# The next tile's second gate/up pair at the end of a round, the decay masks later, and other filler products in the first round

## The chip, the cores and the metric

One NeuronCore of a Trainium2 chip runs one program. The metric is the device time of one execution in microseconds, median of several runs. TensorE is called PE in the views, VectorE DVE, ScalarE ACT, GpSimd POOL and SyncE SP.

## The reference

Two layers over 2 x 1024 tokens of 256 channels, all in float32. Cut to what matters:

```python
xn = layernorm(x)
s = rwkv_attention(xn)          # mixes w,k,v,r,g; decays exp(-exp(w)); recurrence over time per head; W_o
g = silu(down(sparsify_2to4(silu(xn @ w_gate) * (xn @ w_up))))     # of 4 neighbours the 2 largest |h| stay
x = x + s * g
xn = layernorm(x)
s = ssd(xn)                     # B, C, X and a residual gate; chunked scan with decays; w_out
g = silu(down(silu(xn @ w_gate1.T) * (xn @ w_up1.T)))
x = x + s * g
```

## The kernel before

The 2048 tokens are eight tiles of 256. The program runs nine **rounds**. In a round the first layer works on tile `a` and the second layer on the tile before it, `b`. The first round has only `a`, the last only `b`. Rounds two to seven are one hardware loop (`Fori`, line 359), round eight is the same code written out once more with the next tile left out, and `rounds` (line 356) calls `one(a, b)` of each engine. The order of the work on each engine is written by hand in that function, and the engines meet at semaphores.

**The hidden layer of tile `a`** has 1024 units in four pairs of blocks, p0 to p3. `project_p(a, n, "g")` and `"u"` are the gate and up products of pair n: four 128x256 products each, which the records show as eight, because a float32 product leaves two records. ACT makes silu of the gate (`ffn_tanh`, line 574) and DVE multiplies with the up product (`hidden`, line 889). For a pair that `whole` (line 303) doesn't name, ACT makes only a tanh, and DVE needs two instructions (lines 900 and 904) in place of one (896). Then ACT takes the absolute value (`ffn_abs`), DVE compares neighbours (`sparse_compare`, line 1085) and selects, and PE multiplies with the down weights (`down_0`, in the first round `down_part`, line 1540). In the loop, pair 0 of the next tile is made at the end of a round (`next_gate_0`, `next_up_0`), and pair 1 in the middle of the tile's own round, behind `carries`.

**The decays within a tile** are seven levels: `level_next` (line 972) on DVE scales keys and queries, PE multiplies them (`low_levels`, `high_levels`, line 1595), and DVE takes the products under a mask (`own_taken`, `low_taken`, `high_taken`: lines 992 to 1068). In the first round `level` and `level_step` do it step by step in place, and PE has so little to do between them that `kept_at_work` (line 1898) puts products there that nobody reads: one of 256 columns ahead of `level(a, 1)`, one ahead of `out_turned` and six ahead of `turned_1`.

**The second layer's decay rows** `cs_row` come back from DRAM by a DMA, and POOL masks them with an `affine_select` (line 553) that waits for that DMA alone. `end_args` on DVE and `L_exps` on ACT wait for the mask (`cs_masked`). ACT copies B and C into `BC` with sixteen instructions (`bc`, line 602).

**PSUM** has eight banks. `FILLS` (line 54) says which product comes into which bank in what order, `LAST_FILLS` and `FIRST_FILLS` for the last and first round. A product waits until the one ahead of it in its bank is freed. So the tables set which engine a product can wait for.

```python
def kept_at_work(name, count):
    open_bank(a, name)
    for _ in range(count):
        t_.matmul(ps(a, name)[:, 0:C], ident[:, :], W["f_gate"][:, 0:C], start=True, stop=True)
```

## Time and profile before

| what | value |
|---|---|
| runs | 735.85 us median of 3, 734.74 to 736.4 |
| profiled execution | 735.66 us, its span 733.9 us |
| PE | 711.3 us busy (97%), 6896 records |
| PE weight loads | 590.1 us (80%) |
| DVE, ACT, POOL | 497.5 (68%), 342.0 (47%), 77.2 us (11%) |
| mean granted PE clock | 0.995 of full speed |

The span runs from the first to the last instruction. The 1.8 us around it belong to the start and end of an execution. All times below are microseconds from the start of the span. PE's records overlap, so the start of one group to the start of the next is the better measure of its cost.

### The profile page before, as it was taken

Reading aid. Unit: us, or ns where it says so; the run is one execution under the profiler, and the core shown is the slowest. Engines: PE = TensorE matmul, PEld = TensorE weight load, DVE = VectorE, ACT = ScalarE, POOL = GpSimd, SP = SyncE. Lnnn points to the kernel's source line nnn. Section 1 sums busy time; section 2 is a strip of 40 time slices with the busy share of each in tenths; the row PEclk is TensorE's granted clock in tenths of the full one; section 3 lists DMA queues with packets and bytes.
Section 4 is the critical chain, followed back from the end, with each engine's and each line's share of the span. In section 5 each row is a group of like instructions: output and inputs, shape, how many; then the busy total and the mean of one; then the engine's idle time right before and its main releaser. Section 6 shows DMA issues by size and latency. Waiting matters only on the chain.

```text
span 733.9 us, 17949 instructions
## 1 busy us (share of the span) xinstructions
PE 711.3 (97%) x6896; PEld 590.1 (80%) x6896; DVE 497.5 (68%) x1207; ACT 342.0 (47%) x678; POOL 77.2 (11%) x85
## 2 busy tenths in 40 slices
PE   5998999999999999999999999999999999999998
PEld 3777688877888688886888868888788878888686
DVE  4976599547895478955787558855689547895133
ACT  1411685226832468215762168522584236821690
POOL 6301011101011010100111001110101101011020
PEclk9989999999999999999999999999999999999999
DMA  7900351125400353013531145102540136301360
GB/s 238 404 23 29 102 88 32 15 73 144 75 2 15 88 146 59 2 28 104 117 59 16 30 138 95 32 15 69 142 80 3 15 87 145 59 2 26 119 116 16
DMA packets 122444, 55.93 MB, mean 76 GB/s; under 512 B 104384, under 2 KB 114176, under 8 KB 120832
## 3 DMA queue, kind: packets, MB, share of 16 engines
q1 hardware_dynamic: 122368, 54.76, 30.3%
q8 instruction: 66, 1.08, 0.6%
q14 instruction: 10, 0.08, 0.0%
HBM read 42.35 MB, written 12.40 MB: 75 GB/s over the span
## 4 chain that ended last, share of the span: by engine, by line
PE 76%; DVE 12%; issue 5%; DMA 2%; SPq 2%; ACT 2%; POOL 1%; DVEq 0%; ACTq 0%; POOLq 0%
PE psum L1486 58%; PE psum L1707 2%; PE psum L1722 2%; PE psum L1514 2%; PE psum L1565 1%; PE psum L1760 1%; PE psum L1931 1%; PE psum L1595 1%; PE psum L1733 1%; DVE beats L1085 1%; PE psum L1577 1%; DVE own L992 1%; PE psum L1554 1%; PE psum L1873 1%; SPq L453 1%
## 5 line engine op out<-in xcount | busy, mean ns | idle before, releaser
L602 ACT ACTIVATE BC<-psum 64x256 f32<-64x256 f32 x128 | 81.4, 636 | 3.0 <-PE psum L1486 1.3
L1486 PE MATMUL psum<-xn1T,sb_n_gate 128*128 128x256 f32 x256 | 61.3, 382 | 0.0
L1486 PE MATMUL psum<-xn1T,sb_n_up 128*128 128x256 f32 x256 | 60.6, 380 | 0.4 <-DVE cs_row L1294 0.4
L1486 PE MATMUL psum<-xnT,sb_f_gate 128*128 128x256 f32 x240 | 58.5, 386 | 0.0
L1486 PE MATMUL psum<-xnT,sb_f_up 128*128 128x256 f32 x240 | 57.6, 382 | 0.0
L733 ACT ACTIVATE thFB<-psum 128x512 f32<-128x512 f32 x8 | 4.8, 597 | 104.9 <-PE psum L1486 104.9
L1486 PEld LDWEIGHTS psum<-xn1T,sb_n_up 128*128 128x128 f32 x256 | 48.0, 190 | 6.9 <-DVE cs_row L1294 0.8
L1486 PEld LDWEIGHTS psum<-xn1T,sb_n_gate 128*128 128x128 f32 x256 | 48.0, 190 | 6.8
L1486 PEld LDWEIGHTS psum<-xnT,sb_f_up 128*128 128x128 f32 x240 | 44.8, 190 | 6.4 <-issue 0.3
L1486 PEld LDWEIGHTS psum<-xnT,sb_f_gate 128*128 128x128 f32 x240 | 44.2, 189 | 6.8 <-issue 0.2
L1486 PE MATMUL psum<-sb_f_down,hid 128*128 128x256 f32 x224 | 49.5, 379 | 0.0
L1486 PE MATMUL psum<-sb_n_down,hidB 128*128 128x256 f32 x224 | 49.5, 379 | 0.0
L1486 PEld LDWEIGHTS psum<-sb_f_down,hid 128*128 128x128 f32 x224 | 42.6, 190 | 5.8
L1486 PEld LDWEIGHTS psum<-sb_n_down,hidB 128*128 128x128 f32 x224 | 42.6, 190 | 5.8
L553 POOL TENSOR_SCALAR_AFFINE_SELECT cs_row<-cs_row 128x2048 f32<-128x2048 f32 x8 | 16.5, 2062 | 225.7 <-DMA cs_row<-cs_dram 225.7
L628 ACT ACTIVATE cs_row<-cs_row,cs_col 128x128 f32<-128x128 f32 x128 | 38.9, 392 | 0.0
L559 POOL TENSOR_TENSOR cs_half<-cs_half,BC 128x1024 f32<-128x1024 f32 x8 | 18.9, 2363 | 169.5 <-ACT cs_half L697 169.5
L1085 DVE TENSOR_TENSOR beats<-habs 128x768 bf16<-128x768 f32 (+2 forms) x48 | 32.6, 719 | 0.4 <-ACT habs L589 0.4
L1486 PE MATMUL psum<-sb_w_X,xn1T 128*128 128x512 f32 x64 | 31.7, 618 | 0.0
L1486 PE MATMUL psum<-xn1T,sb_w_B 128*128 128x256 f32 x128 | 30.9, 385 | 0.2
L580 ACT ACTIVATE thB<-psum 128x512 f32<-128x512 f32 x32 | 18.8, 594 | 21.8 <-PE psum L1486 21.7
L1486 PE MATMUL psum<-xn1T,sb_w_C 128*128 128x256 f32 x128 | 28.9, 379 | 0.0
(257 smaller groups left out, 1459.0 us busy)
## 6 DMA issues: line engine op xcount, KB each, us to landing
cs_row<-cs_dram SPq DMA_DIRECT2D x8, 1024.0 KB, 4.9
x_dram<-gate SPq DMA_DIRECT2D x8, 512.0 KB, 2.8
cs_half<-cs_dram SPq DMA_DIRECT2D x16, 256.0 KB, 5.9
hidB<-x_dram SPq DMA_DIRECT2D x8, 512.0 KB, 5.9
b_dram<-B_turned SPq DMA_DIRECT2D x32, 128.0 KB, 3.3
hidB<-b_dram SPq DMA_DIRECT2D x8, 512.0 KB, 4.2
X<-in_x SPq DMA_DIRECT2D x9, 256.0 KB, 3.5
XT<-in_x_turned SPq DMA_DIRECT2D x8, 256.0 KB, 3.6
```

What stands on the lines that cost most here:

```text
L453: sp_.dma_start(to[s, e], B_turned[r:r + 32, :].rearrange("p (n d) -> p n d", d=32)).then_inc(B_stored, 16)
L553: g.affine_select(out=cs_row[:, :, :], in_=cs_row[:, :, :], compare_op=ALU.is_ge, fill=NEG, base=0, pattern=[[0, NQ * SCH], [1, P]], chann ...
L559: g.tensor_tensor(cs_half[:, :], cs_half[:, :], BC[:, 1, :, :].rearrange("p t h -> p (t h)"), ALU.mult).then_inc(Cdec_ready, 1)
L580: free(a_.activation(buf[:, :], ps(t, name + "g")[:, :], ACT.Silu), t, name + "g")
L602: ins = a_.activation(cols[:, par, 2 * pair:2 * pair + 2, :], src[64 * par:64 * par + 64, :, s, :], ACT.Identity)
L628: ins = a_.activation(cs_row[:, n, :], cs_row[:, n, :], ACT.Exp, bias=cs_col[:, n:n + 1])
L992: return d.copy_predicated(odd, masks[:, 0, :].rearrange("p (e g b) -> p e g b", e=2, b=32), data)
L1085: did(d.tensor_tensor(beats[:, first:first + count, :], habs[:, i:i + 1, :].to_broadcast([P, count, T]), habs[:, i + 1:4, :], ALU.is_ge))
L1486: ins = t_.matmul(ps(t, name)[first_row:first_row + rows, col:col + n], w, x, start=(k == 0), stop=(k == len(ws) - 1))
L1514: ins = t_.matmul(ps(t, name)[:, i * T:(i + 1) * T], W[w][:, c:c + P], xnT[:, h, 1:T + 1], start=(h == 0), stop=(h == CH - 1))
L1707: ins[s] = t_.matmul(ps(t, names[s])[:, i * P:(i + 1) * P], Bf[r, c * P:(c + 1) * P], Cf[r, c * P:(c + 1) * P], start=True, stop=True)
L1722: t_.matmul(y_out(t, s, c, par), Xrow[:, s, c, :], m[:, par, :], start=(c == 0), stop=(c == 0), skip_group_check=True)
```

## The change

It makes both products of pair 1 of the next tile at the end of a round, behind those of pair 0, also in the first round, where they stand in the place of six filler products. ACT makes silu of both pairs there (`next_gates`) and loads the table for exp, so DVE needs one instruction for pair 1. The bank tables give `p1g` and `p1u` the ends of banks 7 and 4, and `k` moves to bank 2. POOL's mask waits for `level_next(a, 3)` as well, `end_args` moves behind `B_by_block`, and ACT's `gate_tanh` behind the first half of `L_exps`. All three compares of the first half come early on DVE. On PE `res0` stands ahead of `gate_in`. In the first round the down products are cut in pairs of blocks and spread, and the fillers are 128 columns wide, four and nine of them. The differences and `xxxT` (`rank_inputs`) are two functions now, with `normed_1` between them in the first round. In the last round `B0` stands ahead of `carries`.

```diff
-         ["p0g", "mix_k", "w1", "p1g", "mix_g1", "L1", "M1", "kv", "p3u", "yT"],
+         ["p0g", "mix_k", "w1", "mix_g1", "L1", "M1", "kv", "p3u", "yT"],
...
-            return name not in ("p0", "p1", "p2") or (name == "p2" and t.first) or (name == "p0" and not t.first)
+            return name not in ("p0", "p1", "p2") or t.first == (name == "p2")
...
                     pool.wait_ge(cs_rows_loaded, b.count(16, 32))
                     pool.sem_inc(passed, 1)
+                    if a:
+                        pool.wait_ge(lev_ready, a.count(6, 4))
+                        pool.sem_inc(passed, 1)
...
+                def next_gates():
+                    for n in range(2):
+                        ffn_tanh(a.next(), f"p{n}", th[n], None)
+                    exp_tables()
...
                 if a and b:
-                    ffn_tanh(a, "p0", th[0], th_ready)
-                    exp_tables()
                     rank_tanh()
...
-                    gate_tanh()
                     end_exp()
                     L_exps(0)
+                    gate_tanh()
...
+                    if a.reg is not None:
+                        next_gates()
...
                     ffn_tanh_0()
+                    next_gates()
                     copy(a, xn1T[:, :, :], "xT1", CH)
...
                     hidden_p(a, 0)
+                    hidden_p(a, 1)
                     mix_scaled(a, "w")
...
-                    hidden_p(a, 1)
+                    compare(0)
                     mix_g_scaled(a)
                     mix_add(a, "g")
-                    sparse_compare(a, 0, 0)
...
-                    end_args()
                     B_by_block(0)
                     B_by_block(1)
+                    end_args()
...
                     res_gate(1)
-                    sparse_compare(a, 0, 1)
-                    sparse_compare(a, 0, 2)
                     B_decayed()
...
-                        t_.matmul(ps(a, name)[:, 0:C], ident[:, :], W["f_gate"][:, 0:C], start=True, stop=True)
+                        t_.matmul(ps(a, name)[:, 0:P], ident[:, :], W["f_gate"][:, 0:P], start=True, stop=True)
...
                     carries()
-                    project_p(a, 1, "u")
-                    project_p(a, 1, "g")
                     keys()
...
                     low_levels(a)
+                    ssd_proj(b, "res0", "w_res", 0)
                     gate_in()
-                    ssd_proj(b, "res0", "w_res", 0)
...
                         next_up_0()
+                        ffn_p(a.next(), 1)
...
-                    kept_at_work("p2u", 1)
+                    kept_at_work("p2u", 4)
...
-                    kept_at_work("yT", 1)
+                    kept_at_work("yT", 9)
...
                     next_up_0()
-                    kept_at_work("xT1", 6)
+                    ffn_p(a.next(), 1)
                     turned_1()
```

TensorE at the end of the first round, before and then of the change. `sb_f_gate` and `sb_f_up` with `xnT` are a pair's products, `ident` with `sb_f_gate` is the filler, `habs` the transposes of `turned_1`:

```order
L1486 MATMUL psum<-xnT,sb_f_up 128x256 x4
L1903 MATMUL psum<-sb_f_gate,ident 128x256 x6
L1554 MATMUL psum<-ident,habs 128x128 x4
L359 UNCONDITIONAL_BRANCH
L359 ISA
```

```order
L1500 MATMUL psum<-xnT,sb_f_up 128x256 x4
L1500 MATMUL psum<-xnT,sb_f_gate 128x256 x4
L1500 MATMUL psum<-xnT,sb_f_up 128x256 x4
L1568 MATMUL psum<-ident,habs 128x128 x4
L362 UNCONDITIONAL_BRANCH
```

The two groups of pair 1 stand where the six fillers stood.

TensorE in the loop round behind the decay product of the first layer (`decT`), before and then of the change. `prefix,before` is `carries`, `mixed_k` the keys, `mixed_v` the values:

```order
L1807 MATMUL psum<-decT,sb_dec 128x128 x4
L1486 MATMUL psum<-prefix,before 128x2
L1475 REGISTER_ALU
L1486 MATMUL psum<-xnT,sb_f_up 128x256 x4
L1486 MATMUL psum<-xnT,sb_f_gate 128x256 x4
L1813 REGISTER_ALU
L1486 MATMUL psum<-mixed_k,sb_w_rkvgo 128x256 x4
```

```order
L1821 MATMUL psum<-decT,sb_dec 128x128 x4
L1489 ISA
L1500 MATMUL psum<-prefix,before 128x2
L1827 REGISTER_ALU
L1500 MATMUL psum<-mixed_k,sb_w_rkvgo 128x256 x4
```

The pair's eight products have gone from between `carries` and the keys.

VectorE in the loop round from the end of `own_taken` (`same`) to `level_next(a, 4)`, before and then of the change. `B_turned` is `B_by_block`, and `cs_col` and `to_end` are `end_args`, which waits for the mask:

```order
L1068 COPY_PREDICATED own<-same,psum 128x256
L334 REGISTER_ALU
L334 REGISTER_ALU [waits freed2]
L1266 ISA [waits freed3]
L1267 TENSOR_SCALAR cs_col<-cs_pos 128x16 [waits cs_loaded]
L1270 TENSOR_TENSOR to_end<-cs_row,cs_col 128x16 [waits cs_masked,dve_step]
L334 REGISTER_ALU
L334 REGISTER_ALU [waits freed5]
L1277 STREAM_TRANSPOSE B_turned<-BC 128x512 [waits freed6]
L1277 STREAM_TRANSPOSE B_turned<-BC 128x512 [waits freed5,freed6]
L982 TENSOR_TENSOR xn<-thB,dec 128x16x16 [waits lev_ready]
```

```order
L1079 COPY_PREDICATED own<-same,psum 128x256
L337 REGISTER_ALU [waits freed2]
L337 REGISTER_ALU [waits freed3]
L1290 STREAM_TRANSPOSE B_turned<-BC 128x512 [waits freed5,freed6] x2
L1279 ISA
L1280 TENSOR_SCALAR cs_col<-cs_pos 128x16 [waits cs_loaded]
L1283 TENSOR_TENSOR to_end<-cs_row,cs_col 128x16 [waits cs_masked,dve_step]
L993 TENSOR_TENSOR xn<-thB,dec 128x16x16 [waits lev_ready]
```

The two turns of B stand ahead of the instruction that waits for the mask.

## Rows read from the trace of the kernel before

**Rows 1.** The page: busy times, and the granted TensorE clock in 40 slices.
```profile
PE 711.3 (97%) x6896; PEld 590.1 (80%) x6896; DVE 497.5 (68%) x1207; ACT 342.0 (47%) x678; POOL 77.2 (11%) x85
...
PEclk9989999999999999999999999999999999999999
```

**Rows 2.** Waits of TensorE: who for whom, us in total, times, longest.
```profile
PE psum L1486 <- DVE own L1068: 1.6, 7, 0.3
...
PE psum L1749 <- DMA xn1T<-n_dram: 0.9, 1, 0.9
...
PE psum L1776 <- ACT aT_dtT L636: 0.7, 1, 0.7
...
PE psum L1486 <- DVE prefix L1247: 0.6, 1, 0.6
```

**Rows 3.** TensorE, first round, levels: start, duration, what, idle before and its releaser.
```profile
31.30 0.59 PE L1903 MATMUL psum<-sb_f_gate,ident 128*128 128x256 f32 x2
32.58 0.67 PE L1595 MATMUL psum<-rT,kT 64*64 64x32 f32 x32 [0.69 <-DVE rT L969]
33.87 0.71 PE L1577 MATMUL psum<-aT_dtT,sb_mix2b 32*128 32x128 f32 x8 [0.62 <-DVE own L1068]
34.51 2.08 PE L1514 MATMUL psum<-xnT,sb_f_up 128*128 128x256 f32 x4
```

**Rows 4.** One stretch: length, busy PE, PEld, DVE, ACT, POOL; clock, DMA share, GB/s.
```profile
34.50:41.30 6.80, 6.80 (x50) 4.71 (x49) 4.49 (x12) 0.00 (x0) 0.00 (x0) 0.50 0.40 147
```

**Rows 5.** TensorE, first round, its last third.
```profile
49.60 0.63 PE L1859 MATMUL psum<-ident,kT 128*128 128x128 f32 x4 [0.63 <-DVE kT L968]
50.92 0.69 PE L1873 MATMUL psum<-v,mixed_w 128*64 128x64 f32 x16 [0.69 <-ACT mixed_w L593]
...
66.88 1.90 PE L1486 MATMUL psum<-xnT,sb_f_up 128*128 128x256 f32 x8
68.61 2.75 PE L1903 MATMUL psum<-sb_f_gate,ident 128*128 128x256 f32 x12
71.98 0.66 PE L1554 MATMUL psum<-ident,habs 128*128 128x128 f32 x4 [0.62 <-DVE habs L873]
72.47 1.03 PE L1760 MATMUL psum<-mixed_w,sb_w_mix 128*128 128x256 f32 x4
```

**Rows 6.** VectorE: end of the first round, and beside the first mask.
```profile
70.40 0.88 DVE L1127 SCALAR_TENSOR_TENSOR mixed_w<-dxT,sb_vecs,xnT 128x256 f32<-128x256 f32 x2
...
93.29 2.75 DVE L1085 TENSOR_TENSOR beats<-habs 128x768 bf16<-128x768 f32 x1
```

**Rows 7.** TensorE, a loop round: its start, the wait for `own`, high levels, next start.
```profile
161.46 1.13 PE L1760 MATMUL psum<-mixed_w,sb_w_mix 128*128 128x256 f32 x4
...
189.58 1.99 PE L1486 MATMUL psum<-mixed_g,sb_w_rkvgo 128*128 128x256 f32 x8 [0.22 <-DVE own L1068]
...
196.76 0.67 PE L1595 MATMUL psum<-thFB,xn 64*64 64x32 f32 x32
...
197.85 2.00 PE L1486 MATMUL psum<-xnT,sb_f_gate 128*128 128x256 f32 x8
...
248.99 1.13 PE L1760 MATMUL psum<-mixed_w,sb_w_mix 128*128 128x256 f32 x4
```

**Rows 8.** VectorE, the same round: the last low level is taken.
```profile
195.87 0.50 DVE L999 COPY_PREDICATED own<-masks,psum 128x128 f32<-128x128 int8 x2
```

**Rows 9.** ScalarE, the same round: copies of B and C, gate, exps.
```profile
182.94 10.40 ACT L602 ACTIVATE BC<-psum 64x256 f32<-64x256 f32 x16
193.37 0.60 ACT L690 ACTIVATE gT<-psum 128x512 f32<-128x512 f32 x1
...
193.97 2.44 ACT L628 ACTIVATE cs_row<-cs_row,cs_col 128x128 f32<-128x128 f32 x8
```

**Rows 10.** Lines 941 and 553: duration in ns, minimum, median, maximum of eight.
```profile
L941 DVE TENSOR_TENSOR mixed_g<-mixed_g,xnT x8: 692/1144/1516, 35.8 to 617.6; 128x512 f32<-128x512 f32 x8
...
L553 POOL TENSOR_SCALAR_AFFINE_SELECT cs_row<-cs_row x8: 2004/2004/2468, 92.8 to 697.9; 128x2048 f32<-128x2048 f32 x8
```

More of the change, by code:

```diff
@@ L48 @@
 FEAT = {"w": 0, "k": 1, "v": 2, "r": 3, "g": 4}
-FILLS = [["mix_w", "dw", "w0", "k", "mix_g0", "L0", "M0", "k0T", "p3g", "F0"],
-         ["p0g", "mix_k", "w1", "p1g", "mix_g1", "L1", "M1", "kv", "p3u", "yT"],
-         ["p0u", "mix_r", "p1u", "r", "D0", "g", "p2g", "Y0", "s0"],
+FILLS = [["mix_w", "dw", "w0", "mix_g0", "L0", "M0", "k0T", "p3g", "F0"],
+         ["p0g", "mix_k", "w1", "mix_g1", "L1", "M1", "kv", "p3u", "yT"],
+         ["p0u", "mix_r", "k", "r", "D0", "g", "p2g", "Y0", "s0"],
          ["a", "mix_v", "v", "D1", "p2u", "Y1"],
-         ["csum", "C1", "sc0", "st", "n0u", "n2u", "F1"],
+         ["csum", "C1", "sc0", "st", "n0u", "n2u", "F1", "p1u"],
          ["dt", "B0", "res0", "sc3", "n0g", "n2g", "s1"],
          ["X0", "B1", "res1", "sc1", "ys1", "n1u", "n3u"],
-         ["X1", "C0", "sc2", "ys0", "n1g", "n3g"]]
+         ["X1", "C0", "sc2", "ys0", "n1g", "n3g", "p1g"]]
 BANKS = len(FILLS)
@@ L78 @@
                ["a", "mix_v", "v", "p3u", "Y1"],
-               ["p0g", "w0", "D0", "mix_g0", "g", "xT1"], ["p0u", "w1", "D1", "mix_g1", "F0"], ["p1g", "p2g", "yT"], ["p1u", "p2u", "s0"]]
+               ["p0g", "w0", "D0", "mix_g0", "g", "next_p1u"], ["p0u", "w1", "D1", "mix_g1", "F0"],
+               ["p1g", "p2g", "yT", "xT1"], ["p1u", "p2u", "s0", "next_p1g"]]
 FIRST = {n: (b, i + 1) for b, names in enumerate(FIRST_FILLS) for i, n in enumerate(names)}
 EXTRA = [len(names) - (PER[b] if b < RING else 0) for b, names in enumerate(FIRST_FILLS)]
-FILLED_BEFORE = [EXTRA[b] + (NT if b < RING else NT - 1) * PER[b] for b in range(BANKS)]
+FILLED_BEFORE = [EXTRA[b] + (NT if b < RING else NT - 1) * PER[b] - (b in (BANK["p1g"], BANK["p1u"])) for b in range(BANKS)]
 class Tile:
@@ L103, in place @@
         b = BANK[name]
-        return b, self.count(PER[b], NTH[name] + EXTRA[b])
+        behind = 2 if name in ("p1g", "p1u") else 0
+        return b, self.count(PER[b], NTH[name] + EXTRA[b] - behind * PER[b])
     def at(self):
@@ L749, in one @@
                     decay_exp()
-                    ffn_tanh(a, "p1", th[1], th_ready)
+                    ffn_abs(a, 1)
                     copy(a, kT[:, :, :], "k", CH)
@@ L753, in one @@
                     copy(a, v[:, :, :], "v", NQ)
-                    ffn_abs(a, 1)
                     receptances()
@@ L898, in hidden @@
                     return
-                dve.wait_ge(ready, t.count(2, n + 1 if t.first else n))
+                dve.wait_ge(ready, n + 1 if t.first else t.count(1, 2))
                 free(d.scalar_tensor_tensor(out=buf[:, :], in0=buf[:, :], scalar=1.0, in1=ps(t, name + "g")[:, :],
@@ L1124, in differences, with rank_inputs @@
                 did(d.tensor_tensor(dxT[:, :, :], xnT[:, :, 0:T], xnT[:, :, 1:T + 1], ALU.subtract))
+            def rank_inputs(t):
                 after()
@@ L1397, in one @@
                     differences(a.next())
+                    rank_inputs(a.next())
                     result()
@@ L1431, in one @@
                     sparse_compare(a, 1, 0)
+                    sparse_compare(a, 1, 1)
                     states_0()
-                    sparse_compare(a, 1, 1)
                     sparse_compare(a, 1, 2)
@@ L1444, in one @@
                     normed_1()
+                    rank_inputs(a.next())
                 else:
@@ L1465, in _ @@
             differences(Tile(None, 0, first=True))
+            rank_inputs(Tile(None, 0, first=True))
             rounds(dve, one)
@@ L2041, in one @@
                     level_last(a)
-                    keys_turned()
-                    chunk_states()
                     pe.wait_ge(loads["down0"], 16)
@@ L2046, in one @@
                     open_bank(a, "F0")
-                    down_part(a, 0, 0, 4)
+                    down_part(a, 0, 0, 2)
+                    keys_turned()
+                    down_part(a, 0, 2, 4)
+                    chunk_states()
+                    down_part(a, 1, 0, 2)
                     outputs()
-                    down_part(a, 1, 0, 4)
-                    kept_at_work("yT", 1)
+                    down_part(a, 1, 2, 4)
+                    kept_at_work("yT", 9)
                     pe.wait_ge(sparse_ready, a.count(2, 2))
@@ L2069, in one @@
                     X1()
+                    ssd_proj(b, "B0", "w_B", 0)
                     carries()
-                    for name, w in (("B", "w_B"), ("C", "w_C")):
-                        for half in range(2):
-                            ssd_proj(b, f"{name}{half}", w, half)
+                    ssd_proj(b, "B1", "w_B", 1)
+                    for half in range(2):
+                        ssd_proj(b, f"C{half}", "w_C", half)
                     ffn_n(b, 0)
```

## The prediction

> **What bounds the kernel now.** I read the page first. TensorE is busy 711.3 of 733.9 us, and no other engine above 68% [rows 1]. So the time is what TensorE has to do, plus its holes. The clock row stands at full speed but for two slices near the start. The view of waits then says who makes the holes: in all seven rounds that have both tiles it waits 0.2 to 0.3 us for DVE's `own` (1.6 us), and single waits of 0.9, 0.7 and 0.6 us stand at the round seams [rows 2]. The timeline of the first round shows the rest: holes of 0.69 and 0.62 us between small products at 32 us, and of 0.63 and 0.69 us at 50 us [rows 3, 5]. Right behind the first two the granted clock is 0.50 from 34.5 to 41.3 us, that is 1.2 GHz, and TensorE is busy all of that stretch [rows 4]. Last come the round starts. From 72.47 to 161.46 the first loop round takes 88.99 us, the next one 87.53 [rows 5, 7]. In a loop round TensorE is full, so moving work within it gains nothing by itself. Gains come from the first round, from the seams and from the small waits.
>
> **1. The pair in the place of the fillers.** A group of eight records of a pair takes 66.88 to 68.61 = 1.73 us, so the pair costs 3.46 us. Before, the stretch from 68.61 to the start of the transposes at 71.98 holds 12 unread records and a wait of 0.62 us [rows 5]. Now it holds the pair, up to 68.61 + 3.46 = 72.07. That is 0.1 us later, and the wait is gone: `normed_1` on DVE doesn't follow the 0.88 us of `xxxT` any more [rows 6] and is ready earlier. The same pair is no longer in the middle of the following rounds. Every loop round makes one pair, as before, and the eighth makes none. So 3.46 - 0.1 = **3.4 us** go for good. The bank of `p1g` is freed by the residual, which reads it just ahead of 68 us, so this has about 0.8 us of room by the timeline.
>
> **2. The down products in the holes of the first round.** Two blocks' down products (four records, 4 x 0.216 = 0.86 us) go ahead of the key transposes and between these and the states, where TensorE waited 0.63 and 0.69 us [rows 5]. Not all of 1.32 us comes back: the states need ACT's copy of the transposed keys, about 0.6 us, and the outputs need DVE's states behind that. Following the chain the outputs start at 52.9 for 53.46. I take **0.5 us** of 0 to 1.3. Nine narrow fillers ahead of `out_turned` are 18 records of about half the 0.216 us, 1.9 us, in a hole that lasts until DVE has selected. They fit with about 0.5 us left.
>
> **3. The first loop round** falls to the length of the others: 88.99 - 87.53 = 1.46 us. Its 0.7 us wait for `aT_dtT` [rows 2] was ACT, which made silu and loaded a table ahead of `rank_tanh`. This is now done in the round before. Another part is DVE's compare of 2.75 us [rows 6] beside POOL's mask. I take **1.4 us** of 1.0 to 1.8.
>
> **4. The wait for `own`.** With `res0` ahead of `gate_in`, 1.8 us of products stand in the 0.22 us hole [rows 7], and there are seven: 1.6 us [rows 2]. I take **1.4 us** of 0 to 1.6, since the gain is lost where the next wait is as long. That next wait is the point to look at. With the pair gone, all behind `carries` comes 3.46 us earlier on TensorE. Most of DVE and ACT comes with it, because it follows from TensorE's products: `receptances`, then ACT's 10.40 us of B and C copies [rows 9], then the exps. `gate_tanh` is now behind eight exps, 2.44 us [rows 9]. Before, it started at 193.37. Now it starts at 193.37 - 3.46 + 2.44 + 0.3 for `end_exp` = 192.65, and with 0.60 for itself and 0.68 for DVE's product the bank is free at about 193.9. `project_p(a, 2, "g")` wants this bank at 197.85 - 3.46 - 0.22 = 194.2 [rows 7]. So 0.3 us of room is left, where 0.9 were. The masks under low levels end at 195.87 + 0.50 = 196.37 for TensorE's 196.76 [rows 7, 8], a room of 0.39 us, and both move by about the same.
>
> **5. The mask and the compares.** `mix_add` for g takes 692 ns alone and up to 1516 beside the mask, median 1144, and the mask is 2004 ns [rows 10]. Now the mask starts behind `level_next(a, 3)`, beside masked copies and the turns of B. Nothing waits for DVE there but what term 4 prices, so I count nothing. If the cover is gone it costs what rival C says. On DVE the whole first compare moves ahead of the levels, 1.0 us more there, but the second instruction for pair 1 goes, 0.7 us, and the wait for ACT behind `receptances` hides both.
> First the row: an add of two operands in SBUF is slowed by the mask, and the products with PSUM beside it aren't. The Trainium skill, page "SBUF — State Buffer", section "Who interferes with whom", says that a DVE instruction with two SBUF inputs contends with a GpSimd instruction that reads SBUF, and one with a single SBUF input outside the two-port modes does not. The trace agrees for the add; a masked copy beside a POOL instruction is in no row. By the rule the new place costs nothing.
>
> **6. The clock.** The stretch at 1.2 GHz holds 6.8 us of gapless work [rows 4]; at 2.4 GHz it is 3.4 us. Ahead of it stand one filler (0.59 us with its tail), the 0.69 us hole, small products on a quarter of the array, and the 0.62 us hole [rows 3]. Now four fillers of half width take twice that time, some 0.4 us of the first hole, and end ahead of the wait's end. In the trace the fall stands nowhere else, and it comes behind the weakest stretch that TensorE has, so I expect that a fuller one keeps 2.4 GHz. DVE's levels follow at once, since they wait for these products, but its own work becomes the limit in places: **3.0 us** of 0 to 3.4. This is the least sure term.
> The Trainium skill, page "TensorE: Matmul & The Clock Gate", section "Why this matters for your kernels", speaks against it: it asks for no long idle gaps between bursts, and a hole of 0.69 us isn't one. By that rule this filler would change nothing, and the time would be rival A's. The trace disagrees so far, as the clock did fall there.
>
> **7. The last round.** `B0` fills the 0.6 us wait of `carries` [rows 2], but the chain that ends last there is the DMA chain of the sums and of B, and `carries` starts about 1.1 us later. The sums were held on SP's queue for about 1 us anyway. So **0.1 us** is lost, of 0 to 0.6. The wait of 0.9 us for `xn1T` at that seam [rows 2] stays, as nothing ahead of it changes.
>
> **Sum.** 3.4 + 0.5 + 1.4 + 1.4 + 3.0 - 0.1 = 9.6 us. The profiled execution took 735.66 us, and its span 733.9. 735.66 - 9.6 = 726.1, where the median of before is 735.85.
>
> **Rivals.**
> - **A, the clock falls all the same**, there or in a neighbouring stretch. For it: one more 0.4 us of product is little, and the 0.62 us hole stays. Against it: the holes at 50 us brought no fall. It gives 726.1 + 3.0 = 729.1.
> - **B, a new wait in each loop round.** The pair was 3.46 us of cover. Where a chain on ACT or DVE doesn't move with it (the cap is the gate's 0.3 us of room in term 4), TensorE waits. At 0.5 us in each of seven rounds it is 3.5 us: 729.6. With A as well, 732.6.
> - **C, slower: the mask holds the masked copies of `own_taken`.** If these wait for the mask's whole 2.0 us as the add did, less the room of 0.39 us [rows 7, 8, 10], each round loses 1.6 us. That is 11.3 us in seven, with the longer first mask of 2468 ns 11.7, and 726.1 + 11.7 = 737.8. It turns slower by more than 0.2% from a hold of 2.0 us in each round. Against it: masked copies read their data from PSUM, and products with one operand in PSUM weren't slowed.
> - **D, the change does nothing** that can be seen: it would need term 1 to come back in the rounds, 3.5 us, with A and B. 735 to 736.
>
> **Chances.** Forecast (724 to 728) 0.50; A alone 0.24; B alone 0.11; A and B 0.06; C 0.06; D 0.03. The range takes the forecast's own bounds and A, and reaches to B: the low end is 726.1 with terms 2, 3, 4 and 6 at their best (0.8 + 0.4 + 0.2 + 0.4 = 1.8), 724.3, taken as 724.0. The high end is 731.0, between B and the two together. A measurement can tell about 0.2% (1.5 us) from no change. Faster by more than that: forecast, A, B, and A with B, 0.91. Within: D, 0.03. Slower: C, 0.06.
>
> **What would show it.** Right: no stretch at 0.50 clock behind the warm-up; `turned_1` without a wait; start of the second round at about 69 us (72.47 - 3.0 - 0.5 + 0.1); loop rounds of 87.2 to 87.3 us, the first one too; no wait for `own` in `gate_in`; `mix_add` for g at 0.69 us in every round. Term 1 is wrong if the second round's start moves by more than 0.3 us beyond what terms 2 and 6 give. A shows in the clock row. B shows as a wait of TensorE that wasn't there, above all ahead of `project_p(a, 2, "g")`. C shows in `own`'s copies at over 1 us. The prediction is wrong at its root if the loop rounds get longer than 87.6 us.

## The result: slower by 0.36%, where 1.3% faster was forecast

The changed kernel takes 737.01 us (median of 20 runs, 734.08 to 740.88), the kernel before 735.1 us beside it (20 runs, 732.04 to 737.07). The ratio is 1.0036, with a 95% interval of 1.0021 to 1.0051. The forecast was 726.1 us in a range of 724 to 731. So it is about 11 us off, on the wrong side. The profiled execution of the changed kernel took 737.69 us, its span 735.9.

The page of the changed kernel, the rows that answer to [rows 1], and the row of the queue that loads instructions (packets, MB, share):

```profile
PE 710.0 (96%) x6906; PEld 589.9 (80%) x6906; DVE 489.0 (66%) x1200; ACT 343.5 (47%) x678; POOL 76.4 (10%) x85
...
PEclk9999999999999999999999999999999999999999
...
q8 instruction: 66, 1.08, 0.6%
```

TensorE is busy for 1.3 us less, the slice at a lower clock is gone, and yet the span is 2 us longer. The waits of TensorE answer to [rows 2]:

```profile
PE psum L1763 <- issue: 6.7, 5, 1.6
PE psum L1500 <- DVE cs_row L1307: 1.8, 1, 1.8
```

The loop's waits for `own` and the one for `aT_dtT` are gone, as forecast. In the first place stands something new: five times TensorE is idle at line 1763, 6.7 us in all, and the releaser is "issue", that is nothing that the profile shows. Line 1763 is the step product of the second layer, in the third group of products that a loop round makes. Two stretches of the changed kernel, the first loop round and the second (length, busy PE and so on, as in [rows 4]):

```profile
69.83:157.46 87.63, 87.33 (x860) 73.03 (x860) 61.44 (x152) 42.66 (x85) 7.42 (x5) 1.00 0.28 65
157.46:246.62 89.16, 87.53 (x859) 73.02 (x860) 60.70 (x150) 42.24 (x85) 7.41 (x5) 1.00 0.27 64
```

The first loop round, which is entered from above, takes 87.63 us. The next five, entered by the loop's jump back, take 89.16, 89.20, 89.38, 89.31 and 88.90, where before they took 87.53 (161.46 to 248.99, [rows 7]) and on average 87.38. That is 9.05 us of loss in five rounds. The stall itself is 6.7 of these. The rest doesn't stand as idle time of its own, and the runs below say only in part where it goes. Everything else went the way that was forecast: the second round starts at 69.83 for 72.47 [rows 5] (-2.64), the first loop round is 1.36 shorter, and from the start of the eighth round to the end it takes 132.48 for 135.53 (-3.05). -2.64 - 1.36 + 9.05 - 3.05 = +2.0, the difference of the spans. The second round was forecast to start at about 69 us. Part of its delay isn't the change: TensorE came to its full rate later in this profile. An equal group of four records takes 1.50 us here (14.16 to 15.66) and 1.06 in the kernel before (14.08 to 15.14), and the group of four from 11.2 us on takes 1.9 in both.

The stall itself, TensorE at the start of the third loop round of the changed kernel (start, duration, what, idle before):

```profile
246.62 1.13 PE L1774 MATMUL psum<-mixed_w,sb_w_mix 128*128 128x256 f32 x4
...
247.94 0.27 PE L1763 MATMUL psum<-xn1T,sb_w_dt 128*32 128x128 f32 x1
...
249.64 0.41 PE L1763 MATMUL psum<-xn1T,sb_w_dt 128*32 128x128 f32 x3 [1.33 <-issue]
```

It stops in the middle of one projection: four records of its group have the same operands and the same bank, and after the first of them TensorE stands still for 1.33 us. No semaphore stands there. What does stand there, as the experiments show, is an edge in the instruction stream. The queue q8 brings TensorE's instructions in pieces of 16384 bytes, and the places of the stalls below fit 256 instructions in each. A piece is said to be asked for when its transfer starts on q8. In this round one is asked for at 243.77, the next at 247.10, and TensorE goes on at 249.64, 2.54 us behind that.

### The profile page after: what moved, and what is told of

It is laid out like the page before. It is cut to its first block, busy times and chain, and to the rows that moved or that the text cites. A ratio compares the mean times of both kernels' runs of the same rounds, so it can differ in the third digit from the quotient of the medians.

```text
span 735.9 us, 17879 instructions
## 1 busy us (share of the span) xinstructions
PE 710.0 (96%) x6906; PEld 589.9 (80%) x6906; DVE 489.0 (66%) x1200; ACT 343.5 (47%) x678; POOL 76.4 (10%) x85
## 4 chain that ended last, share of the span: by engine, by line
PE 85%; DVE 5%; issue 4%; DMA 2%; SPq 2%; POOL 1%; ACT 0%; DVEq 0%; POOLq 0%; ACTq 0%
PE psum L1500 64%; PE psum L1609 3%; PE psum L1721 2%; PE psum L1736 2%; PE psum L1528 1%; PE psum L1774 1%; PE psum L1579 1%; PE psum L1945 1%; PE psum L1747 1%; PE psum L1642 1%; PE psum L1591 1%; SPq L445 1%; SPq L456 1%; PE psum L1887 1%; PE psum L1568 1%
## 5 line engine op out<-in xcount | busy, mean ns | idle before, releaser
L927 DVE SCALAR_TENSOR_TENSOR mixed_w<-psum,sb_vecs,dxT 128x256 f32<-128x256 f32 x16 | 7.0, 479 | 41.8 <-PE psum L1579 41.8
L907 DVE SCALAR_TENSOR_TENSOR hid<-th,psum 128x512 f32<-128x512 f32 x23 | 15.7, 686 | 24.0 <-PE psum L1500 24.0
L586 ACT ACTIVATE th<-psum 128x512 f32<-128x512 f32 x23 | 13.7, 598 | 37.7 <-PE psum L1500 29.7
L1500 PE MATMUL psum<-xn1T,sb_w_res 128*128 128x256 f32 x128 | 30.8, 385 | 0.0
```

What stands on the lines that cost most here:

```text
L586: free(a_.activation(buf[:, :], ps(t, name + "g")[:, :], ACT.Silu), t, name + "g")
L907: free(d.scalar_tensor_tensor(out=to, in0=buf[:, :], scalar=2.0, in1=ps(t, name + "u")[:, :], op0=ALU.mult, op1=ALU.mult), t, name + "u")
L1500: ins = t_.matmul(ps(t, name)[first_row:first_row + rows, col:col + n], w, x, start=(k == 0), stop=(k == len(ws) - 1))
```

## The experiments

**How the places are counted.** In the built program a float32 matmul is four instructions; a wait or a register operation is one. So the first instruction of the loop can be numbered: 1161 in the kernel before, 1213 in the changed one, because this has 13 matmults more in the first round (the pair and the narrower fillers). If the edges between pieces stand at 1250 (give or take one) plus or minus multiples of 256, the stall above is at one, 37 instructions behind the loop head. The loop is 1816 instructions long in the changed kernel and 1820 in the one before. The experiments in the table moved the loop head against the edges and left the loop's code alone. The edit is a number of increments of a semaphore that nobody reads, at the start of TensorE's program, where it waits for its first data, and a change in number and width of the unread fillers at about equal columns:

```diff
             t_ = nc.tensor
+            for _ in range(30):
+                pe.sem_inc(passed, 1)
...
-                    kept_at_work("yT", 9)
+                    kept_at_work("yT", 13, 88)
```

(`kept_at_work` takes the width as a third argument in these.) "Round" is the mean of the five rounds entered by the jump, in the profiled execution. Pieces are those of q8. In b_pad52, c_pad20, c_less20, a_pad204 and e_head_at_m3 one, one, one, two and four of these rounds also hold a stretch of 3.41 us at 1.2 GHz, which stands behind a stall.

```
kernel           loop head  instructions from  pieces  round   stall behind    time
                            head to next edge  in all   us     the jump, us     us
before             1161            89            66    87.38      none        735.1
changed            1213            37            66    89.19   1.07 to 1.65   737.01
a_pad64            1277           229            66    87.50      none        732.55
a_pad128           1341           165            66    87.56      none        744.77
a_pad204           1417            89            67    90.12   elsewhere      775.21
b_pad52 (before)   1213            37            66    89.86   1.56 to 1.94   747.31
c_pad20            1233            17            66    89.66   1.32 to 1.87   740.36
c_less20           1193            57            66    89.09   elsewhere      738.55
e_head_at_m3       1247             3            66    91.40   2.42 to 2.69   747.78
e_head_at_1        1251           255            21    86.95      none        723.67
c_moved46          1259           247            21    86.93      none        723.65
e_head_at_21       1271           235            66    87.46      none        730.05
d_before_moved     1259           247            30    87.01      none        733.27
```

### Is it the place of the code?

> The changed kernel with 64 instructions more on TensorE's queue at the very start of the program (increments of a semaphore that nobody reads; TensorE has nothing to do there until 14 us). The loop's code is the same, it only stands 64 instructions later. Theory (instruction fetch): the 1.33 us in which TensorE stands still behind each back-jump of the loop is a late 16 KB piece of its instructions, and whether it is late depends on where the loop head stands in a piece. Then the stall goes in all five rounds that are entered by the jump: 5 x 1.3 to 1.6 us less, 737.0 - 7 = 730 us, later loop rounds at 87.6 us instead of 89.2. Rival (a wait of the changed order, for a semaphore or a bank, that the profile doesn't show): nothing changes, 737 us and rounds of 89.2.

> The changed kernel with 128 such instructions ahead. Instruction fetch: again another place of the loop head (half a piece on), no stall, 730 us, unless the jump back itself now meets another piece's edge. Rival of a hidden wait: 737 us. [...]

> The changed kernel with 204 = 256 - 52 such instructions ahead. The change put 52 instructions more ahead of the loop (13 matmults of four instructions), so with a piece of 256 the loop head now stands in a piece as in the kernel before. Instruction fetch: no stall, as in the kernel before, 730 us. Rival of a hidden wait: 737 us.

> The kernel before, all its work the same, with 52 such instructions ahead of TensorE's, so that its loop head stands in a piece as in the changed kernel. Instruction fetch: the stall of 1.3 to 1.6 us appears behind the five back-jumps, 735.1 + 7 = 742 us, loop rounds of 88.8 us instead of 87.3. Rival of a wait of the changed order: the kernel stays at 735.1 us.

**Measured.** a_pad64: 732.55 us, ratio 0.9973 (0.996 to 0.9986). The same loop, 64 instructions further down, has rounds of 87.50 us and no stall, and a_pad128 has 87.56 and none. So a round of the changed kernel loses 1.69 us by its place, 1.35 of them idle at the stall. The two also show that without the stall the new order has rounds no shorter than the 87.38 of the kernel before; 87.2 to 87.3 were forecast. b_pad52: 747.31 us, ratio 1.0186 (1.0157 to 1.0214). The kernel before, not changed in its work, gets the stall of the changed one, at the same product:

```profile
251.70 0.28 PE L1768 MATMUL psum<-mixed_w,sb_w_mix 128*32 128x128 f32 x2
253.70 0.41 PE L1751 MATMUL psum<-xn1T,sb_w_dt 128*32 128x128 f32 x3 [1.72 <-issue]
```

So the rival, a hidden wait of the new order, falls: the stall can be given to the old order and taken from the new one. Two things were not as expected. The increments cost 0.15 us each, and TensorE's first product starts at 7.5 us and not at 14, so only some 34 of them fit ahead of it. With 52, 64, 128 and 204 of them it starts at 10.19, 12.03, 21.80 and 33.53 us, so these four times hold up to 26 us that have nothing to do with the loop. And a_pad204, which I had put at no stall since its head stands in a piece as in the kernel before, has one elsewhere. TensorE at the end of its low levels (before this row 28 of the 32 records of the group are done):

```profile
305.11 0.30 PE L1611 MATMUL psum<-xn_turned,thB 64*64 64x32 f32 x4 [1.86 <-issue]
```

These four records are two products, instructions 2021 to 2028; the edge is at 1250 + 3 x 256 = 2018, one product ahead. The 256 instructions ahead of it are almost only products of the low levels, which run at 15 ns a record, and TensorE has done them in less time than the next piece takes to come: it was asked for 2.6 us ahead of the row's start. So there are two kinds of such a stall: behind a jump, and behind a run of very short instructions.

### How long is it, and what does it depend on?

> The changed kernel with 20 increments at the start, so that the first edge of a piece stands 17 instructions behind the loop head and not 37. Instruction fetch: TensorE goes on 3.0 us after the round's first product whatever it has done until then (249.64 - 246.62 in the changed kernel, of which 1.33 us idle). Up to the edge it has 0.9 us of work and not 1.7, so the stall is 2.1 us and the rounds are 0.8 us longer, 90.0 us; time 737 + 4 = 741 us. If the place of the edge doesn't matter: 737.

> The changed kernel with the fillers ahead of out_turned as 4 of 256 columns in place of 9 of 128, 20 instructions fewer ahead of the loop, so that the first edge of a piece stands 57 instructions behind the loop head. Instruction fetch: 2.8 to 2.9 us of work stand ahead of the edge, so only 0.1 to 0.3 us of stall are left of 1.33, rounds of 88.0 us, and 737 - 6 = 731 us. If the place of the edge doesn't matter: 737.

**Measured.** c_pad20: 740.36 us for 741 expected. That the time was met is in part luck, since all five runs have a mean clock of 0.993 to 0.997, where 14 of the changed kernel's 20 have 0.999 or more. The stall moved to the place forecast, 17 instructions in, one projection earlier:

```profile
247.64 0.41 PE L1782 MATMUL psum<-mixed_w,sb_w_mix 128*32 128x128 f32 x3
249.37 0.27 PE L1782 MATMUL psum<-mixed_w,sb_w_mix 128*32 128x128 f32 x1 [1.32 <-issue]
```

It is shorter than I wrote (1.32 to 1.87 for 2.1). From the round's first product to the end of the stall it is 2.76 to 3.53 us over the twenty stalls behind a jump in the changed kernel, b_pad52, c_pad20 and e_head_at_m3, so that stretch isn't fixed. From the piece's request to TensorE going on it is 2.15 to 2.87 us in the same twenty. c_less20 was expected at 731 us and took 738.55. The stall behind the jump is gone, as expected, but the edge at 1762 now falls into the last low level, and there are 0.60 to 1.71 us of stall there, in every round:

```profile
271.45 0.43 PE L1609 MATMUL psum<-xn_turned,thB 64*64 64x32 f32 x12
273.04 0.54 PE L1609 MATMUL psum<-xn_turned,thB 64*64 64x32 f32 x20 [1.16 <-issue]
```

The kernel before has an edge at nearly the same place of its low levels and no such stall. There the piece was asked for at 272.29, 1.8 us ahead of the group, in c_less20 at 270.41, 1.1 us behind its start. Why it was asked for so much earlier there I can't say.

### The version that beats both

> The changed kernel with its loop head 46 instructions later, at no cost: 30 increments at the start, where TensorE has 5.1 us to spare (0.15 us each), and the fillers ahead of out_turned as 13 of 88 columns in place of 9 of 128. The first edge of an instruction piece then stands 247 instructions behind the loop head and no longer 37. Instruction fetch: no stall in the loop, rounds of 87.5 us as with 64 increments, but without that kernel's 4.5 us later start: 732.55 - 3.6 (the first back-jump came that much later there) = 729 us. A hidden wait of the changed order would give 737.

**Measured.** 723.65 us (722.97 to 724.97, 4 runs), ratio 0.985 (0.9815 to 0.9885), 5 us better than expected. The page's rows, and the same stretch of the loop as above:

```profile
PE 705.7 (98%) x6914; PEld 589.1 (81%) x6914; DVE 488.6 (68%) x1200; ACT 343.4 (47%) x678; POOL 77.2 (11%) x85
...
q8 instruction: 21, 0.34, 0.2%
```

```profile
156.64:243.57 86.93, 86.65 (x861) 72.81 (x859) 60.71 (x149) 42.27 (x85) 7.41 (x5) 1.00 0.28 64
```

21 pieces in place of 66, and none between 125 and 590 us: the loop is loaded once and then held. Its 1816 instructions are 7.1 pieces, and its head is 9 behind an edge, so it touches eight pieces, 2048 instructions. Its rounds agree within 0.04 us, where they scatter by 0.3 to 0.5 us in the kernel before and in the changed one. Part of what is won stands at the jump itself: from the start of the last group of products of a round to the first product of the next it is 1.73 us in e_head_at_1, which is held too (328.38 to 330.11), 1.92 in the kernel before (334.31 to 336.23) and 2.26 in e_head_at_21, which is loaded in each round (329.57 to 331.83). The Trainium skill, page "Runtime: NRT & Kernel Launch", section "Instruction fetch mechanics", states the size: 128 KiB or 2048 instructions for TensorE, refilled in blocks of 16 KiB or 256 instructions. The pieces of q8 and the loop held in eight of them agree. The same section calls this memory two lines only, and the runs disagree for TensorE. It calls the cost of crossing an edge mostly hidden. That holds for most of the 66 pieces of the changed kernel, but not for the five behind a jump. I had not weighed this page for the prediction.

> The changed kernel with 38 instructions more ahead of the loop (34 increments at the start, the fillers ahead of out_turned as 10 of 115 columns), so that the loop head is 1 instruction behind an edge. The loop then ends 25 instructions into its eighth piece. Theory (ring of eight pieces): the loop is held, some 21 instruction pieces in all, rounds of 86.9 us, 723.7 us. If only the one place of c_moved46 works, pieces are loaded in each round and the time is over 730.

> The same with 30 increments, four instructions fewer: the loop head is now 3 instructions ahead of an edge, and the loop touches nine pieces. All its work and its order are the same as in e_head_at_1. Theory: it isn't held, 66 pieces are loaded, and behind each back-jump TensorE gets 3 instructions of the head and stands until the next piece comes, a stall longer than the 1.3 to 1.9 us at 17 instructions: 2 to 2.8 us, rounds of 90 us, 742 to 748 us. If four instructions can't matter: 723.7 us.

**Measured.** These two differ by four increments of a semaphore that nobody reads. 723.67 us (ratio 0.9862, 0.983 to 0.9893) against 747.78 us (1.0193, 1.0158 to 1.0228). 24 us hang on four instructions. With the head 3 ahead of an edge, one product of the round runs and then TensorE stands, and the waits show it (two of the seven are short ones):

```profile
PE psum L1776 <- issue: 13.0, 7, 2.7
```

```profile
160.64:164.05 3.41, 3.41 (x13) 1.18 (x4) 0.00 (x0) 1.44 (x4) 0.00 (x0) 0.50 0.07 13
```

The second fence is a stretch of that kernel: 1.3 us behind the end of the stall of 2.50 us at 159.38 the granted clock is 0.50 (1.2 GHz) for 3.41 us. So a stall can cost twice: the four rounds with such a fall take 91.5 to 92.0 us, and the one without, behind a stall of 2.50 us as well, takes 89.82. That is 87.3, 2.5 for the stall and some 2 for the clock. Shorter stalls bring it too, but not each time. Of the 21 stalls of over 1.5 us within the loops of these kernels 10 have a fall behind them, the shortest of these being 1.58 us in c_pad20. In the changed kernel the stalls of 1.07 to 1.65 us brought none in the profile, though 6 of its 20 runs have a mean clock below 0.999.

> The changed kernel with 58 instructions more ahead of the loop (34 increments at the start, the fillers ahead of out_turned as 15 of 77 columns): the loop head is 21 instructions behind an edge, and the loop ends 45 instructions into its eighth piece. If the next piece is asked for only further in, the loop is held: 21 pieces, rounds of 86.9 us, 723.7 us. If it is asked for within 45 instructions of the edge, the head's piece is lost: 66 pieces, rounds of 87.5 us as with 64 increments, and without that kernel's late start 728 to 729 us.

**Measured.** 730.05 us, 66 pieces. A loop that reaches 33 instructions into its eighth piece is held (c_moved46), and so is one that reaches 37 (d_before_moved, below); one that reaches 45 isn't. The reading that fits is that the next piece is asked for somewhere between, and that it takes the place of the head's; no view shows which piece is which. All four runs have a mean clock of 0.997 or 0.998. In the profile the fall stands at 707.28 us, behind a wait of 2.5 us for `cs_row` in the last round, so the time is somewhat more than the loop's loading costs.

### Is the change itself worth anything?

> The kernel before, all its work the same, with its loop head 98 instructions later and so 9 instructions behind an edge of a piece, as in c_moved46: 26 increments at the start, and the six fillers of 256 columns ahead of turned_1 as 24 of 64. In c_moved46 no instruction piece at all was loaded from 125 to 590 us: the loop stays in the instruction buffer, 7.1 pieces long, if it ends 33 instructions into its eighth piece; with 64 increments it ended 51 into it and every round loaded eight or nine pieces. Here the loop is 4 instructions longer and ends 37 into its eighth piece. Theory: it is held as well, rounds of 86.9 to 87.0 us in place of 87.35, first loop round shorter too, 735.5 - 3 = 732.5 us or less; the change at an equal place of the code is then worth 732 - 723.65 = 8 to 9 us. Rival: the gain of c_moved46 comes from the changed order alone, and the kernel before stays at 735 with pieces loaded in each round.

**Measured.** 733.27 us beside 733.53, ratio 0.9999 (0.9982 to 1.0016). The loop is held as expected (30 pieces, none from 220 to 593 us, rounds of 87.01 us for 87.38), but the time, expected at 732.5 us or less, doesn't follow: the second round starts at 72.87 us, with a stretch at 1.2 GHz (34.95 to 38.36 us) ahead of it, and by how much the 24 narrow fillers add to that was not tried alone. The first of its five rounds still loads seven pieces (161.7 to 219.9 us) and takes 87.03 us like the others. So loading as such costs nothing there. The rounds say it better. With both loops held, the change brings 87.01 to 86.93 us in the five rounds, 88.05 to 87.22 in the first loop round, and 135.63 to 131.88 from the start of the eighth round to the end. That is 0.4 + 0.8 + 3.75 = 5.0 us behind the second round's start. The medians, 733.27 and 723.65, are 9.6 us apart, and the profiled spans 8.4, of which 3.45 stand ahead of the second round.

> c_moved46 with gate_in ahead of res0 again, as in the kernel before; the number of instructions stays. Term 4 of the prediction says 0.2 us more in each of seven rounds, 723.65 + 1.4 = 725.1 us. Against it: with res0 ahead, 0.15 us more went by ahead of the high levels and the outputs, which took back most of it; then 723.7 to 724.2.

> c_moved46 with carries ahead of B0 in the last round again, as in the kernel before. In the profiles of the changed order TensorE waits 1.2 to 2.0 us there for the decay rows ahead of the second layer's gate products, 0.35 in the kernel before. If B0 ahead of carries delays the sums and with them the DMA of the decay rows by 1.1 us, this wait shrinks by 0.8 us and the time to 723 us. If the wait is for other work, 723.65 or 0.5 us more, since carries then waits 0.6 us again.

**Measured**, both against c_moved46 (723.65). d_gate_first swaps two lines:

```diff
-                    ssd_proj(b, "res0", "w_res", 0)
                     gate_in()
+                    ssd_proj(b, "res0", "w_res", 0)
```

725.03 us (724.61 to 725.97). Its rounds are 86.98 us for 86.93, so the trace gives `res0` ahead of `gate_in` 0.35 us in seven rounds, where the medians give 1.4. Within this spread the term is 0.35 to 1.4 us. d_old_tail puts `carries` ahead of `B0` again in the last round: 723.52 us, the same. By the traces the stretch from the eighth round on is 132.17 us for 131.88, so the change of order there gains 0.3 us, if anything. The wait for `cs_row` is 0.9 us there for 1.2, so it is only in small part due to `B0`.

> c_moved46 without GpSimd's new wait for level_next(a, 3): the mask runs as soon as its DMA is in, as in the kernel before. If its place matters for the time (the add for g slowed from 0.69 to 1.5 us beside it), 723.65 + 0.5 or more. If DVE's work there is covered, 723.65 with the add at over 1 us. The first loop round is where it could show, since there it lay beside the compare as well.

```diff
-                    if a:
-                        pool.wait_ge(lev_ready, a.count(6, 4))
-                        pool.sem_inc(passed, 1)
```

**Measured.** 735.92 us (735.16 to 737.51): 12 us more, with the loop held as well (21 pieces). I had expected half a microsecond at most. GpSimd's mask and what runs beside it on VectorE, in this kernel, and then the same step in c_moved46, where the mask waits:

```profile
176.26 2.00 POOL L556 TENSOR_SCALAR_AFFINE_SELECT cs_row<-cs_row 128x2048 f32<-128x2048 f32 x1 [33.30 <-DMA cs_row<-cs_dram]
```

```profile
176.49 2.05 DVE L990 TENSOR_TENSOR mixed_w<-kT,dec 128x256 f32<-128x256 f32 x1 [1.05 <-ACT rT L686]
```

```profile
174.92 0.43 DVE L993 TENSOR_TENSOR mixed_w<-kT,dec 128x256 f32<-128x256 f32 x1 [1.05 <-ACT rT L689]
```

```profile
183.38 0.67 PE L1608 MATMUL psum<-xn_turned,thB 64*64 64x32 f32 x32 [0.65 <-DVE xn_turned L992]
```

With the pair gone from the middle of the round, all of VectorE's work comes earlier, and the mask, which comes when its DMA is in, no longer hits `mix_add` for g but the first product of the levels. That takes 1551 to 2247 ns in the six rounds from 176 us on, for 427. The levels are a chain, TensorE waits for them (last row), and the five rounds are 1.8 us longer on average. One of them (89.90 us) has a fall of the clock as well; the other four are 1.5 us longer.

### The clock

> As the kernel before in this list, loop head at the same place, but the filler ahead of level(a, 1) is again one product of 256 columns and not four of 128. It tells what these fillers do for the clock. If they keep the clock up, it falls here at 34 us for some 6.8 us and the time is 3 us longer (732). If the fall depends on something else (with 52 increments ahead of the kernel before it vanished too), nothing changes: 729.

> The kernel before, not changed, for a second profile of it: does the granted clock fall behind the first small holes each time? If the fall belongs to the work there, it stands again at 34.5 to 41.3 us. If it is a matter of where the holes fall in time (with 52 increments ahead of it, it was absent), the second profile may have it or not, and the start of the second round is then at 72.5 or at 69.4 us.

> The kernel before with its filler ahead of level(a, 1) as four of 128 columns, as in the change, and nothing else (12 instructions more, first edge 77 behind the loop head, so no stall there by the theory). Of 44 runs of the kernel before so far 8 have a mean clock of 0.999 or more, the others a stretch at 1.2 GHz. If these fillers keep the clock up (term 6 of the prediction), most runs are at 1.0 and the median is 1.5 to 2 us lower than before's. If they don't, 1 in 5 as before, and the same time.

**Measured.** c_old_fill has the old filler ahead of `level(a, 1)` and takes 723.64 us, ratio 0.9865 (0.9826 to 0.9904), like c_moved46; its profile shows no fall, and one of its four runs has a mean clock of 0.998. before_again, a second profile of the very kernel before, shows none either. The stretch of [rows 4] in it:

```profile
34.50:41.30 6.80, 6.80 (x118) 5.36 (x117) 5.93 (x17) 1.23 (x2) 0.00 (x0) 1.00 0.54 165
```

Its second round starts at 68.49 us for 72.47, and the execution took 731.33 us for 735.66. e_before_fill, the kernel before with the new filler alone, took 734.26 us beside 733.47, ratio 1.0016 (1.0001 to 1.0032), and its profile has a stretch at 0.50 from 47.29 to 50.70 us, behind the holes that end at 45.7 and 47.0. Of 73 runs of the kernel before beside these experiments 15 have a mean clock of 0.999 or more, with a median of 731.8 us; the other 58 have 734.6. Of the changed kernel's 20 runs 14 have a mean clock of 0.999 or more, of e_before_fill's 12 runs 5. Those 5 have a median of 733.9 us, 2 us more than the 15 of the kernel before, so the new filler, or the 12 instructions by which it moves the loop, costs something of its own. c_old_fill, where the old filler gains nothing, speaks for the place.

## Why the prediction was wrong, point by point

- **The root.** The prediction said that it is wrong at its root if the loop rounds get longer than 87.6 us. They did: 89.19 us on average, where 87.2 to 87.3 were forecast. The missing term is not in its sum at all. The step that failed is that the sum takes the length of a loop round from TensorE's work and its waits for other engines alone, and puts the place of the loop in the instruction stream at nothing, without a reason. The change moved the loop by 52 instructions, and the runs show 9.05 us for it in the profile, of which 6.7 are TensorE standing still for instructions; between two other places of the same loop it is 24 us. The profiled execution is 737.69 - 726.1 = 11.6 us off: 9.05 for this, 1.0 of term 4, which was forecast for these rounds and didn't come, 0.8 at the start of the second round and 0.8 in the first loop round and behind the loop. None of the rivals was this one. Rival B comes nearest, with a new wait in each loop round, but it is a wait for ACT or DVE, at 0.5 us.
- **Term 1, the pair** (3.4 us): right. From the eighth round on 3.05 us less in the changed kernel, 3.65 in c_moved46. At the seam the pair stands in the place of the fillers, and the wait of 0.62 us [rows 5] is gone:

```profile
65.82 1.89 PE L1500 MATMUL psum<-xnT,sb_f_gate 128*128 128x256 f32 x8
67.55 1.89 PE L1500 MATMUL psum<-xnT,sb_f_up 128*128 128x256 f32 x8
69.28 0.60 PE L1568 MATMUL psum<-ident,habs 128*128 128x128 f32 x4
```

- **Term 2, down products in the holes** (0.5 us): 0.3 us. From the first product of the keys in the first round to the transposes for the output it is 35.26 us for 38.70, and 3.1 of these 3.4 us are the clock.
- **Term 3, the first loop round** (1.4 us): 1.36 us. How much of it is ACT's silu and how much the compare beside the mask was not tried.
- **Term 4, `res0` ahead of `gate_in`** (1.4 us): 0.35 to 1.4 us in the held loop, and nothing to be seen in rounds of 87.50 us for 87.38 (a_pad64). The wait for `own` went, 0.28 us a round by the starts of the groups in a_pad64, and there about 0.3 us came back ahead of the high levels and the outputs. The prediction had named this: the gain is lost where the next wait is as long.
- **Term 5, the mask** (0): the sum was right, the reason too weak. The add for g takes 692 ns in every round, as forecast, and `own`'s copies are as fast as before (505 and 443 ns for 503 and 439), so rival C falls. But "I count nothing" missed what the wait is there for: without it the changed order loses 12 us. The rule cited in the prediction was the one that would have told it, applied to another instruction. The Trainium skill, page "SBUF — State Buffer", section "Who interferes with whom", says that a DVE instruction with two SBUF inputs contends with a GpSimd instruction that reads SBUF. The product of `kT` and `dec` has two, and took 2.05 us for 0.43; the masked copies of PSUM have one, and did not slow.
- **Term 6, the clock** (3.0 us): right in size for the two profiles, too large for the median, and its cause isn't shown. Between two profiled runs it was 3.1 us. But the fall comes and goes between executions of one kernel, so its absence in one profile says nothing of the filler that the prediction credited. With this filler alone 5 of 12 runs go without a fall, for 15 of 73, and the time is no lower; so few runs can't tell more. About 2.7 us separate the runs of before without a fall from those with one (731.8, 734.6), and four of five have one, so some 2 us were to be had. That the changed kernel falls less often (6 of 20) is measured; which of its parts does it, the filled holes at 50 us perhaps, was not tried alone.
- **Term 7, the last round** (-0.1 us): within what can be seen, +0.3 by the traces, 0 by the medians. The wait for `cs_row` of 1.8 us that stands there now, 0.4 before, takes back some of term 1 and was not forecast; c_moved46 has 1.2 of it.
- **Rival B**, the gate's room of 0.3 us: no wait stands ahead of `project_p(a, 2, "g")` in the changed kernel.

With its one missing term taken out again, the same change takes 730.05 us in e_head_at_21, whose loop is loaded in each round as that of the kernel before is. That lies in the stated range, 4 us above the forecast. The 723.65 us of c_moved46 are below the forecast, but by a gain that nobody had forecast: its loop is held. The forecast reads most of the work rightly and leaves out where the program stands.

## What to carry to other kernels

A change to the code ahead of a hardware loop also moves the loop in the instruction stream, and that is a variable of its own. Where an engine waits for "issue" at the same instruction each round, look at the q8 row and count the instructions from the loop head to the stall; before a reorder is judged, move the loop by some dozens of instructions, at a place where the engine has time to spare, and take the best place for both kernels. A wait that looks superfluous may hold a slow neighbour away from a chain: take it out alone before it is costed at nothing. And a dip of the clock in one profile is one draw; its frequency is in the clocks of all runs.

## What the runs showed of the hardware

- TensorE's instructions come in pieces of 16384 bytes. Each took 0.9 to 1.5 us on its queue as a rule, and TensorE went on 2.15 to 2.87 us after the transfer of the one that it lacked had started (twenty stalls behind a jump, four kernels).
- A loop of 1816 instructions was held, with no load for 465 us, when its head stood 1 or 9 instructions behind an edge, and was loaded anew in each round at 21 or more behind or 3 ahead. Held, its rounds were 0.5 to 0.6 us shorter than loaded without a stall (86.93 and 86.95 for 87.46 to 87.56), and alike to 0.05 us.
- The spread of the times fell with it: 722.97 to 725.62 us in 8 runs of c_moved46 and e_head_at_1, 734.08 to 740.88 in 20 of the changed kernel.
- An increment on TensorE's queue takes 0.15 us where nothing else runs.
- The granted clock fell from 2.4 to 1.2 GHz for 3.41 us behind 10 of 21 stalls of 1.56 to 2.69 us. Behind holes of 0.6 to 0.7 us between small products it fell for 6.8 us in one execution of the kernel before and not at all in another.
